# First three batches of the delta net interleaved with the second half of the expert units, on one core

## The reference, cut to what matters

```python
# experts: g * u, weighted by the routing, summed over e
g = silu(einsum('th,efh->tef', x, w1_e)); u = einsum('th,efh->tef', x, w3_e)
routed = einsum('tef,ehf,te->th', g * u, w2_e, combine)
# delta net, over the time steps of one batch, 16 heads of 8 channels, two memories c
q, k = rope(x @ Wq), rope(x @ Wk); v = x @ Wv           # then elu + 1 on q and k
beta = clip(sigmoid(x @ Wbeta + bbeta), 0.001, 0.999)
M = M * beta[c] + k (outer) v ;  Z = Z * beta[c] + k
num = einsum('bd,bcde->be', q, M); den = einsum('bd,bcd->b', q, Z) + 1e-6
out = num / den;  h = x + out @ Wo + bo;  layernorm of h
```

## Time and profile before

| | us |
|---|---|
| median of three runs | 1560.65 |
| lowest and highest | 1559.08, 1566.92 |
| the profiled execution's time | 1561.28 |
| its span, first to last instruction | 1560.0 |
| DVE busy | 1105.7 (71%) |
| PE busy | 1187.8 (76%) |
| POOL busy, ACT busy | 702.3, 727.1 |
| mean granted TensorE clock | 0.876 |

### The profile page before, as it was taken

How to read it: one execution, slowest core, us unless ns; L and a number is a source line. 1 busy time by engine, 2 the same in 40 slices (tenths; PEclk the granted TensorE clock), 3 DMA queues, 4 the chain that set the end, 5 groups by cost and what they waited for, 6 DMA issues and landing times.

```text
span 1560.0 us, 18619 instructions
## 1 busy us (share of the span) xinstructions
PE 1187.8 (76%) x5568; PEld 541.8 (35%) x5568; DVE 1105.7 (71%) x3003; ACT 727.1 (47%) x1591; POOL 702.3 (45%) x857
## 2 busy tenths in 40 slices
PE   3414987999998578475748688898889898988863
PEld 1212454555554133142412222333333333333222
DVE  5888645755555699888858786787788888887032
ACT  4644783255554200323221166665566556665741
POOL 7334672555455378767660023115321532154244
PEclk9856988999999688787865588999999999999995
DMA  3000105222221000020215200202020302000010
GB/s 106 0 1 0 46 1 126 77 60 65 63 69 33 11 0 1 0 56 0 46 24 86 34 1 4 58 4 48 1 35 4 48 1 36 3 1 4 1 41 13
DMA packets 33666, 47.02 MB, mean 30 GB/s; under 512 B 5007, under 2 KB 18191, under 8 KB 33263
## 3 DMA queue, kind: packets, MB, share of 16 engines
q1 hardware_dynamic: 30974, 43.84, 12.9%
q10 hardware_dynamic: 2592, 2.00, 0.5%
HBM read 39.14 MB, written 6.68 MB: 29 GB/s over the span
## 4 chain that ended last, share of the span: by engine, by line
PE 29%; DVE 24%; POOL 8%; issue 6%; ACT 6%; DMA 0%; ACTq 0%; POOLq 0%; DVEq 0%
PE PS L608 8%; PE PS L566 5%; PE PS L591 5%; DVE PS L1115 4%; DVE SS L1118 4%; DVE RB L1027 3%; DVE RB L1028 3%; PE PS L653 3%; PE PS L271 2%; ACT RB L1507 2%; DVE PS L1016 2%; DVE st L698 2%; POOL RB L1695 1%; POOL RB L1697 1%; PE PS L389 1%
## 5 line engine op out<-in xcount | busy, mean ns | idle before, releaser
L1507 ACT ACTIVATE RB<-PS 128x512 f32<-128x512 f32 (+3 forms) x768 | 328.2, 497 | 266.9 <-PE PS L591 263.3
L566 PE MATMUL PS<-B 96*128 96x512 bf16 (+3 forms) x768 | 259.8, 361 | 54.2 <-DVE B L1161 22.9
L1744 POOL TENSOR_SCALAR_AFFINE_SELECT RB<-RB 128x512 f32<-128x512 f32 x128 | 81.5, 637 | 411.3 <-ACT RB L1507 411.3
L1115 DVE CUSTOM_DVE_ANT_0 PS<-PS,w_msk 128x128 f32<-128x128 f32 (+3 forms) x512 | 243.7, 505 | 30.2 <-PE PS L566 29.7
L591 PE MATMUL PS<-B 96*128 96x512 bf16 (+3 forms) x768 | 240.7, 335 | 18.8 <-ACT RB L1507 17.2
L1118 DVE TENSOR_REDUCE SS<-PS 128x1 f32<-128x512 f32 x256 | 175.5, 686 | 37.6 <-PE PS L566 36.8
L608 PE MATMUL PS<-RB,B 128*32 128x512 f32 (+3 forms) x1536 | 170.7, 517 | 14.4 <-ACT RB L1514 14.4
L566 PEld LDWEIGHTS PS<-B 96*128 96x128 bf16 x768 | 77.1, 101 | 205.5 <-DVE SS L1115 65.9
L1675 POOL TENSOR_TENSOR RB<-RB,B 128x512 f32<-128x512 f32 x64 | 83.8, 1313 | 128.1 <-DVE RB L936 97.6
L472 PE MATMUL PS<-RB,w_hspread 128*128 128x512 f32 x128 | 79.5, 756 | 58.5 <-POOL RB L1697 55.9
L936 DVE TENSOR_TENSOR RB<-RB,PS 128x512 f32<-128x512 f32 x72 | 48.9, 681 | 103.7 <-ACT RB L1365 76.1
(11 more groups left out here) (230 smaller groups left out, 2079.1 us busy)
## 6 DMA issues: line engine op xcount, KB each, us to landing
B<-scrW SPq DMA_DIRECT2D x128, 128.0 KB, 3.0
B<-scrQ SPq DMA_DIRECT2D x72, 128.0 KB
scrQ<-B SPq DMA_DIRECT2D x6, 384.0 KB, 4.1
B<-scrK SPq DMA_DIRECT2D x36, 64.0 KB
X<-in_x SPq DMA_DIRECT2D x8, 256.0 KB, 8.6
out_dram<-X SPq DMA_DIRECT2D x8, 256.0 KB, 3.0
B<-in_w SPq DMA_DIRECT2D x3, 576.0 KB, 4.9
B<-in_zeros SPq DMA_DIRECT2D x9, 128.0 KB
```

The costliest lines, as they stand in the source:

```text
L566: pe.matmul(p[:, 0:w], qs[u % 3][:, h, 128 * i:128 * i + 128], keys_of(u, h)[:, 512 * c:512 * c + w], start=True, stop=True).then_inc(s["m ...
L1115: ins = dve.tensor_tensor_reduce(p, p, msk[:, 512 - w:512], 1.0, LOWEST, ALU.add, ALU.max, MX[:, u % 2, i, h, c:c + 1])
L1507: act.activation(RB[:, 4 * (step % 3) + z, 0:w], bank(bank_of["score", step, z])[:, 0:w], ACT.Exp).then_inc(s["ex2"], 1)
```

## The change

The delta net's loop no longer begins when the experts are through, but when unit 36 of 72 is due. From there each delta step `s` carries two of the experts' `v`, `36 + 2s` and `37 + 2s`: the 36 units left lie in steps 0 to 17, the heads' rest runs on to step 26. Steps 27 to 35 carry only the last batch, and the loop ends after 39 steps instead of 42. The delta unit itself is tighter: sum and query follow in the same step, and `query_c` two steps later.

Since the experts keep rows of `RB`, the memories of the first 20 units lie in parts of the tiles that belong to batch 3 (`CLOSED`), one pair only where two alternated; groups 6 and 7, which fill those parts, wait until unit 20 is through. PSUM is shared out anew: from unit 36 one bank for the first product (4), one for the second (6), 0 and 1 for the value (single until unit 27), 2 and 3 for the query, and bank 7 alone for all heads and passages up to step 26. The experts' result is copied out of PSUM by ACT (`copy_m`), and its norm comes one and two units later on POOL and ACT. On PE the heads' projections now follow a unit's products, and silu comes ahead of the heads' work on ACT. The passage is cut in 15 slices, from step `9b + 10`; each of the three cuttings is one closed sequence (`part_e`), and batch 2 takes them in pairs.

```diff
-        mem0, mem1, msum = [wide(0), wide(2)], [wide(4), wide(6)], [wide(8), wide(10), wide(12)]
-        C_STEPS = 42
-        PASS_AT = [9 * b + 13 for b in range(4)]
-        PASS_SLICES = 11
+        C_STEPS = 39
+        BESIDE = 27
+        ROWS_FROM = 20
+        CLOSED = [batch(B[z], 3) for z in (QD, KD, 3)] + [batch(SS, 3)]
+        def places(n):
+            if n < ROWS_FROM:
+                return 0, 1, 2 + n % 2, 0
+            if n < BESIDE:
+                return 4, 5, 6 + n % 2, 0
+            return (8, 9, (10, 7, 6)[n % 3], 0) if n % 2 else (4, 5, (10, 7, 6)[n % 3], 4)
+        PASS_AT = [9 * b + 10 for b in range(3)]
+        PASS_SLICES = 15
+        PASS_PAIRS = [[0], [1, 2], [3], [4], [5], [6], [7], [8], [9, 10], [11, 12], [13, 14]]
+        ALONE = 36
+        def beside(step):
+            return [v for v in (ALONE + 2 * step, ALONE + 2 * step + 1) if v < MOE_STEPS]
+        def gate_bank(v):
+            return (4 + v % 2) if v < 27 else (4, 1)[v % 2] if v < ALONE else 4
+        def up_bank(v):
+            return (6 + v % 2) if v < 27 else (6, 3)[v % 2] if v < ALONE else 6
+        def out_bank(g):
+            return (0, 2, 0)[g] if g < 3 else 5
 ```

TensorE:

```diff
+            def next_d(v):
+                dbank[0] += 1
+                return 1 + 2 * (dbank[0] % 2) if v < 27 else 7
+            def next_f(step):
+                ring_f[0] += 1
+                return 6 + ring_f[0] % 2 if step >= BESIDE else 7
-            pe.wait_ge(s["beta_d"], 16)
-            pe.wait_ge(s["t_d"], 32)
-            pe.wait_ge(s["a_m"], 72)
-            pe.wait_ge(s["nx"], 16)
-            banks.emptied.clear()
+            value_c(0)
             for step in range(C_STEPS):
-                if 0 <= step - 4 < 36:
-                    query_c(step - 4)
+                if 0 <= step - 2 < 36:
+                    query_c(step - 2)
+                for v in beside(step):
+                    experts(v)
+                if step < 35:
+                    value_c(step + 1)
+                if step % 9 in (4, 5) and step < 36:
+                    weight_c(step // 9, step % 9 - 4, step)
                 for b, k in pass_slices(step):
-                    pass_f(b, k, next_f)
-                if step < 36:
-                    value_c(step)
+                    pass_f(b, k, lambda: next_f(step))
 ```

VectorE:

```diff
             for step in range(C_STEPS):
+                units = [v for v in beside(step) if v < 9 * NG]
+                if step < 36:
+                    value_c(step)
+                    memory_c(step, 0)
+                for v in units[0:1]:
+                    gated_m(v)
+                if step < 36:
+                    memory_c(step, 1)
+                for v in units[1:2]:
+                    gated_m(v)
+                for v in beside(step):
+                    between_m(v)
+                if step % 9 == 2 and step < 36:
+                    weight_c(step // 9)
                 for b, k in pass_slices(step):
+                    pass_f(b, k)
 ```

ScalarE:

```diff
+            def copy_m(g):
+                act.wait_ge(s["o_m"], 9 * g + 9)
...
+                act.activation(rX[g % 2], bank(out_bank(g)), ACT.Copy).then_inc(s["oc_m"], 1)
+            def part_e(b, n, o, rows_, scale):
+                p = bank(bank_of["pj_e", b, n])[0:rows_, :]
+                act.wait_ge(s["pj_e"], 4 * b + n + 1)
+                act.activation(o[:, 0, :], p, ACT.Copy, scale=scale).then_inc(s["r_e"], 1)
+                act.wait_ge(s["cut_e"], 3 * b + n + 1)
+                act.activation(o[:, 1, :], p, ACT.Copy).then_inc(s["cm_e"], 1)
 ```

GpSimd:

```diff
             for step in range(C_STEPS):
+                units = [v for v in beside(step) if v < 9 * NG]
+                for v in units[0:1]:
+                    gated_m(v)
+                if step < 36:
+                    memory_c(step)
+                for v in units[1:2]:
+                    gated_m(v)
+                for v in beside(step):
+                    between_m(v)
                 for b, k in pass_slices(step):
                     pass_f(b, k)
```

## The result

| | us | ratio to the kernel before |
|---|---|---|
| kernel before, median (20 runs) | 1564.53 | 1 |
| changed kernel, median (20 runs) | 1557.03 (1549.27 to 1561.85) | 0.9957 [0.9941, 0.9973] |
| span of the profiled execution | 1554.8, before 1560.0 | |

A forecast was written before the change was run, and what follows sets the result against it. PE was taken to bound the experts' half and DVE the delta net. From unit 36 to the last block 445.5 us (14.5 saved), 3 saved before, 2 lost in the last block: 1546 us from 1561.3, range 1508 to 1585.

The forecast's parts named there:

- the band to which it gave 0.22: Whole kernel: time within about 0.5% (7.8 us) of no change, chance 0.22; faster meant below 1553 us.
- the lock: DVE's SBUF-bound instructions in combined steps wait until POOL's whole instruction ends, some 1.3 us each on average.
- the ladder of single banks: Combined steps: single PSUM banks make PE and DVE wait in turn; with blocking, 12.05 us a step instead of 10.
- the right one: Sign for the forecast: scans about 12 us apart in steps 0 to 9, blocked instructions 1.7 to 2.2 us, clock 0.95 or more.
- the clock rival: Combined steps: PE's granted clock falls to 0.9 or less, 2.5 us a step lost, 1600 us; chance 0.17.
- The full overlap: Rival for the combined steps: blocking and PE's waits mostly hide, 10.5 us a step, 1510 us; chance 0.20.
- POOL come last: Rival: with one memory pair, scans wait for POOL; each batch beside the experts may lose 7 us more, 1560 us; chance 0.15.
- Steps 18 to 26: Heads' rest beside the delta net: 118.5 us, of it 15 (bounds 5 and 25) for bank waits and cuttings.
- Steps 0 to 9: First combined steps of experts, heads and delta net: 116.5 us, or 117.7 from scan to scan; 12.05 a step.
- Steps 10 to 17: Remaining steps with experts' units, plus the first eight slices of batch 0's passage: 114 us.
- Units 0 to 35: Experts' units still run alone: PE's waits shrink by silu's earlier place and later norms, 3 us saved (bounds 0 and 6).
- step 27 to the last block: Last batch and tail: 78 us for steps 27 to 35 and 18.5 of tail; 95.3 from scan to scan.

The follow-up runs named there:

- DVE's edit: Changed kernel with VectorE's head work of a step's first unit moved ahead of the second scan: 1551.63 us, ratio 0.9918.
- mended kernel: Changed kernel with value and head banks alternating from unit 20, and VectorE's and GpSimd's head work of a step's first unit issued earlier: 1529.17 us, ratio 0.9779.
- silu first: Kernel before with one edit: ScalarE's silu issued ahead of the group's end and the head work: 1544.09 us, ratio 0.9885.
- silu late: Changed kernel with ScalarE's silu put back behind the head work in units 0 to 35 alone: 1567.88 us, ratio 1.0026.

## Why the prediction was wrong

**What held, and what was luck.** The time fell, to 1557.0, inside the range, but short of the 1553 from which the prediction counted it as faster; it lies in the band to which it gave 0.22. And it fell by another term than the one forecast: of 14.5 us from unit 36 to the last block nothing came, of 3 us ahead of it 8.4 came. That the direction was right is luck to this extent.

Both mechanisms, the lock and the ladder of single banks, are in the traces; their sizes, and what they were added to, were off. Of the signs, the scans of steps 0 to 9 are 12.1 us apart, as the right one asked. The blocked lines have means of 1.57, 1.43 and 1.68 in steps 0 to 8 (L999, L1007, L1014), longer than the 1.05, 0.95 and 0.78 over the whole kernel before, but short of 1.7 to 2.2. The granted clock is 0.97 in steps 0 to 8, and 0.91 in 9 to 17, between the 0.95 of the right sign and the 0.9 of the clock rival (whose 2.5 us a step are 2.2 by its own numbers, 12.2 less 10.0). The last block begins at 818.1, past 816. The full overlap didn't come: steps average 12.4 and 14.0 us, not 10.5. Nor did POOL come last: from 359 to 597 us DVE has no wait for POOL in its list.

**The steps that failed** are terms of the sum. The part from unit 36 on was given 445.5 us and took 458.8, 13.3 more.

*Steps 18 to 26*, 118.5 forecast, 124.8 measured: the term mis-sized most. The sum had 103.3 us of DVE's own work and blocking, and 15 of waiting for the value's and the heads' ladder and the cuttings (bounds 5 and 25). The stretch shows DVE busy 98.4 us and idle 26.4, beyond the upper bound. With second banks from unit 20 seven of these nine steps lose 13.3 us, and DVE's idle time in them falls from 19.6 to 6.7.

*Steps 0 to 9*, 117.7 forecast, 121.4 measured. The first nine steps were 9.45, 13.13, 14.16, 13.56, 11.45, 8.47, 13.81, 16.53 and 11.23 (forecast 9.1, 13.9, 12.4, 13.7, 11.9, 8.9, 12.5, 13.4, 12.7). The step that is off by 3 lacks a rung: POOL's statistics behind its long operations, then ACT's norm, then silu. The ladder was worked out with PE, DVE and POOL's two long operations; ACT's queue has no term in it, and the copy on ACT was put at nothing because ACT is busy half of the time. With POOL's statistics first that step is 3.5 us shorter, though only 1.0 of it is left at step 9; with DVE's edit beside it the nine steps take 104.1 for 111.8. Steps 10 to 17, 2.3 too short, were not taken apart.

*The lock*, 1.3 us for each of 32 instructions of groups 4 to 7, 42 us: in the changed kernel they lasted 31 longer, 1.0 each, and 10 to 14 reached the end. In the mended kernel it is 24 longer and 22 at the end. The wait for the whole instruction was right, the mean was a quarter less than priced; that all of it reaches the end is shown only where little else is waited for.

*Units 0 to 35*, 3 saved (bounds 0 and 6): 8.4 in the profiles, and the silu's place alone is 10.8 by the medians. The step said that silu ahead of the heads shrinks PE's waits, and capped it by PE's idle time, 7.5 of 127 us. The cap was wrong twice. It was read in units 36 to 71; in units 0 to 35 of the kernel before, the stretch that it was used for, PE is idle for 15.9 of 134.4 us (12.1 of 126.0 in the changed kernel). And a busy time that counts matmuls by their modelled ends hides idle time: with silu first, units 36 to 71 took 10 us less, while PE's idle time fell by 5.6, from 7.5 to 1.9; the other 4.5 is the busy time of the same matmuls, 119.9 and 115.4, both at a granted clock of 1.00. The pitch of the starts had the answer in the prediction's own numbers: a unit is 2.6 and seven ninths of 0.87, 3.28 us. Over the 35 pitches from unit 36 to 71 it was 3.62 in the kernel before and is 3.33 with silu first. With it the rival that was missing: the stage that the change takes apart could be had 16 us shorter by two moved lines.

The last two rows of the table, step 27 to the last block and the last block itself, were right within 1 us each. And the split of the work was good for more than was forecast: 426 us instead of 445.5 in the mended kernel, by banks and order within a step alone.

## What to carry over

Before laying a stage beside another, ask what the stage in turn would take with its own queues in order, and count that as the rival: here one engine's order was worth 18 us, more than twice the whole change. Price an engine's slack by the pitch of its starts, not by its busy share. When two engines hand each other work inside a step, mend all links of the ladder together, since each alone mostly passes the wait on; and before a piece is moved behind another on an in-order queue, ask what that other piece itself waits for.

## What the runs showed beside

The lock works both ways. POOL's L1768 (L1695 in the earlier trace rows, 2.35 us) took 2.71 when it began 0.16 after DVE's L1007 (639.15 and 639.31, above). L1770 took 2.68 to 2.72 in eleven of the steps 0 to 26, and each time it had begun while L999 or L1007 was running; in the other sixteen it took 2.40 to 2.42 when L1012 or L1014 was running, and 2.34 to 2.36 when none of the four was. And the experts' stage varies from one execution to the next: step 0's scan was at 358.1 to 366.6 us in kernels whose instructions up to there are the same, with POOL's waits for the transfer of the routing weights at 20.0 to 26.0 us in all. Two single profiles can't price anything under some 8 us there, so the 8.4 above rests on the timed pair with silu late; the steps behind it agree within 1 us, most within 0.1, but for step 1.
